# Image loops of two stages written out, and a group norm spread over more taps

## What is computed

```python
x = x + L0(_gn(x), ...)   # state space scan over the 4096 positions of half the channels, 3x3 convolution of the rest
x = x + L1(_gn(x), ...)   # four sweeps of a 9-tap convolution, line by line: down, up, right, left
x = x + L2(_gn(x), ...)   # column convolution times a gate of 8 groups
x = x + L3(_gn(x), ...)   # deformable convolution, batch norm, leaky relu

def _gn(v, G=32, eps=1e-5):          # group norm: mean and variance of 4 channels of one image
    g = v.reshape(B_, G, C_ // G, H_, W_)
    return ((g - mean(g)) / sqrt(var(g) + eps)).reshape(v.shape)

# deformable convolution: offsets and mask from a 3x3 convolution of the input; each of 9 taps reads
# four corners at an offset position, weighs them, and a 128x128 product per tap is summed
samp = corner(y0, x0, ...) + corner(y0, x0 + 1, ...) + corner(y0 + 1, x0, ...) + corner(y0 + 1, x0 + 1, ...)
out = einsum('bckhw,ock->bohw', samp * mask, dcn_w)
```

## Time and profile before

| | |
|---|---|
| three runs | 6858.83, 6863.93, 6866.51 us |
| the profiled execution | 6866.86 us, its span 6865.1 us |
| first stage, about 108 to 2118 us | DVE busy 1906 of 2010 us |
| second layer, 2118 to 3690 us | PE busy 1540 of 1572 us |
| preparing image 0, 3690 to 3821 us | PE busy 117 of 131 us |
| sampling, 3821 to 6765 us | 2304 gathers on POOL |
| the end, 6765 to 6865 us | stores and loads |

### The profile page before, as it was taken

The page is one execution under the profiler, slowest core; times in us unless marked ns, Lnnn a source line. Parts: engine busy times, 40 slices in busy tenths (PEclk is TensorE's granted clock), DMA queues, the critical chain, the costliest instruction groups (busy, mean ns, idle before and its releaser), DMA issues. The chain is left out here.

```text
span 6865.1 us, 89120 instructions
## 1 busy us (share of the span) xinstructions
PE 5560.6 (81%) x21147; PEld 3191.4 (46%) x21147; DVE 5515.3 (80%) x12845; ACT 3422.5 (50%) x7221; POOL 4025.5 (59%) x3805
## 2 busy tenths in 40 slices
PE   4999999999998999999998767667676767676542
PEld 2444444444446888888885323333233333333221
DVE  6999999999996777777885777777878787877667
ACT  4888787888885541111111444444444444444333
POOL 3888888888882000010000577777777777777773
PEclk9999999999999999999999988888897989798665
DMA  5455444444443000000000677777777777777777
GB/s 194 174 186 180 174 166 169 164 178 164 174 167 128 3 4 0 0 25 0 0 0 20 187 244 218 238 222 230 227 227 233 221 240 216 243 211 237 213 209 284
DMA packets 306391, 1093.54 MB, mean 159 GB/s; under 512 B 56560, under 2 KB 58639, under 8 KB 264604
## 3 DMA queue, kind: packets, MB, share of 16 engines
q0 software_dynamic: 187440, 625.23, 30.2%
q1 hardware_dynamic: 118516, 464.08, 18.9%
HBM read 997.72 MB, written 91.37 MB: 159 GB/s over the span
## 5 line engine op out<-in xcount | busy, mean ns | idle before, releaser
L1286 POOL DMA_INDIRECT d_ring<-corner_table,d_idx_now x2304 | 2207.7, 958 | 873.0 <-issue 797.4
L983 POOL TENSOR_TENSOR X<-X 128x512 f32<-128x512 f32 x1024 | 1286.2, 1273 | 235.5 <-DVE X L1021 219.2
L1332 ACT ACTIVATE d_mix<-d_ring,d_w_now 128x128 f32<-128x128 f32 x2304 | 735.9, 390 | 1319.7 <-DMA d_ring<-corner_table,d_idx_now 1243.4
L1486 PE MATMUL d_ps_s<-small,d_mix 128*128 128x128 f32 x2304 | 454.7, 330 | 985.9 <-DVE d_mix L1658 969.8
L1021 DVE TENSOR_TENSOR_SCAN X<-X,m_pB 128x512 f32<-128x512 f32 x896 | 1133.2, 1270 | 0.0
L1658 DVE SCALAR_TENSOR_TENSOR d_acc<-d_ring,d_w_now,d_mix 128x128 f32<-128x128 f32 x2304 | 662.7, 355 | 579.4 <-ACT d_mix L1332 559.9
L277 PE MATMUL prop_ps<-prop_parts,prop_w_hi 128*128 128x480 f32 (+4 forms) x4536 | 1097.4, 386 | 4.6 <-DVE prop_parts L286 4.6
L877 PE MATMUL m_pY<-X,small 128*128 128x512 f32 x2048 | 1033.5, 602 | 73.9 <-POOL X L983 73.7
L1486 PEld LDWEIGHTS d_ps_s<-small,d_mix 128*128 128x128 f32 x2304 | 296.1, 164 | 1524.3 <-DVE d_mix L1658 871.4
L277 PEld LDWEIGHTS prop_ps<-prop_parts,prop_w_hi 128*128 128x128 f32 x4536 | 814.8, 188 | 132.8 <-DVE prop_parts L286 5.4
L225 ACT ACTIVATE prop_sum<-prop_ps 128x256 f32<-128x256 f32 x504 | 194.5, 386 | 1166.7 <-PE prop_ps L277 1166.7
(11 more groups left out here) (231 smaller groups left out, 8047.3 us busy)
## 6 DMA issues: line engine op xcount, KB each, us to landing
X<-c_scratch SPq DMA_DIRECT2D x256, 1024.0 KB, 4.8
d_ring<-corner_table,d_idx_now POOLq DMA_INDIRECT x2304, 3.7
corner_table<-d_tT SPq DMA_DIRECT2D x120, 256.0 KB, 3.9
X<-in_x SPq DMA_DIRECT2D x8, 2048.0 KB, 15.2
m_res<-in_x SPq DMA_DIRECT2D x64, 256.0 KB, 4.5
x_scratch<-m_res SPq DMA_DIRECT2D x64, 256.0 KB, 2.1
x_scratch<-X SPq DMA_DIRECT2D x8, 2048.0 KB, 8.7
b_x<-x_scratch POOLq DMA_DIRECT2D x16, 1024.0 KB, 12.9
```

The source lines that it names most:

```text
L983: pool.tensor_tensor(hc[:, n % NHC, :], h[:, n, :], Cb[:, n, :], ALU.mult).then_inc(s.HC, 1)
L1286: pool.indirect_dma_start(out=ring[:, m % RING, :], out_offset=None, in_=flat, in_offset=bass.IndirectOffsetOnAxis(ap=idx_now[:, c % 2, m: ...
L1332: r0 = act.activation(R[:, k % 3, t, :], ring[:, m % RING, 0:P], ACT.Copy, scale=w_now[:, c % 2, 4 * m:4 * m + 1])
L1486: turned = pe.transpose(ps_s[k % 3][:, t, :], R[:, k % 3, t, :], G.ident)
```

## The change

The loops over images become Python loops, so that all images are straight code on every engine: three places. In the preparation, table and offsets begin two slots later (`T_AT` 34 in place of 32); the steps of each norm are at slots 0, 2 and 3 after its first (28, 30, 31, and 68, 70, 71), PE's average stays one slot after the first, ACT's root is three after it. `add_x1` goes from every 5 slots to every 4 (34, 38, ... 62). The averages of the two norms use two banks. Two waits of PE fall away or are replaced.

```diff
-            with eng.Fori(1, B) as b:            # layer0, program: PE, DVE, ACT, POOL
+            for b in range(1, B):
-                with sp.Fori(1 + KEEP, B - 1) as b:
+                for b in range(1 + KEEP, B - 1):
-                with eng.Fori(1, B - 2) as p:    # layers2_and_3, passes: all engines
+                for p in range(1, B - 2):
-    T_AT = NORM_AT + 4
+    T_AT = NORM_AT + 6
-    NORM_STEPS = ((0, 5), (5, 9), (9, GN))
-    ADD_AT = {T_AT - 1 + 5 * i: i for i in range(NCH)}
-    X1_LOAD = {max(0, 5 * i - 6) // 2: i for i in range(1, NCH)}
-    FIRST_NORM_AT = max(T_INDEX) + 1
+    NORM_STEPS = ((0, (0, 5)), (2, (5, 9)), (3, (9, GN)))
+    ADD_AT = {T_AT + NT * i: i for i in range(NCH)}
+    X1_LOAD = {max(0, NT * i - 4) // 2: i for i in range(1, NCH)}
+    FIRST_NORM_AT = max(T_MASK)
+            ps_moments = (ps_c[:, 0:2], ps_a[:, 0:2])
...
-                            if n == NORM_AT + 2:
+                            if n == NORM_AT + 3:
                                 deviation(q, 1)
-                            if s.adding and n == FIRST_NORM_AT + 2:
+                            if s.adding and n == FIRST_NORM_AT + 3:
                                 deviation(q + 1, 0)
...
-                        pe.matmul(ps_c[:, 0:2], G.group_mean, mom[:], start=True, stop=True).then_inc(s_gm, 1)
+                        pe.matmul(ps_moments[which], G.group_mean, mom[:], start=True, stop=True).then_inc(s_gm, 1)
...
                             if n == NORM_AT + 1:
-                                pe.wait_ge(s_math, NM * NCH * s.q + CREDIT)
                                 group_moments(s.q, 1)
                             if s.adding and n == FIRST_NORM_AT + 1:
-                                pe.wait_ge(s_math, NM * NCH * s.q + NM * NCH + CREDIT)
+                                after(pe, s_mask, NCH * s.q + (NCH - 1))
+                                pe.wait_ge(s_math, NM * NCH * s.q + (NM * (NCH - 1) + 1 + CREDIT))
                                 group_moments(s.q + 1, 0)
...
-                            if i == 0:                     # before PE's first turn of the offsets
-                                after(pe, s_gn, GN * 2 * q + (GN + 8))
...
-                            for later, steps in enumerate(NORM_STEPS):
+                            for later, steps in NORM_STEPS:
                                 if n == NORM_AT + later:
                                     image_norm(s.q, 1, *steps)
```

More of the change, by code:

```diff
@@ L1085, in layers2_and_3 @@
     ALL = NCH * TAPS
-    NORM_STEPS = ((0, 5), (5, 9), (9, GN))
-    ADD_AT = {T_AT - 1 + 5 * i: i for i in range(NCH)}
-    X1_LOAD = {max(0, 5 * i - 6) // 2: i for i in range(1, NCH)}
-    FIRST_NORM_AT = max(T_INDEX) + 1
-    assert max(ADD_AT) < FIRST_NORM_AT and FIRST_NORM_AT + 2 < ALL
+    NORM_STEPS = ((0, (0, 5)), (2, (5, 9)), (3, (9, GN)))
+    ADD_AT = {T_AT + NT * i: i for i in range(NCH)}
+    X1_LOAD = {max(0, NT * i - 4) // 2: i for i in range(1, NCH)}
+    FIRST_NORM_AT = max(T_MASK)
+    assert max(ADD_AT) < FIRST_NORM_AT and max(FIRST_NORM_AT + 3, max(T_TABLE) + 3, max(T_INDEX)) < ALL
     with ExitStack() as ctx:
@@ L1585, in image_norm @@
                             after(dve, s_gm, 2 * q + which)
-                        do(5, lambda: dve.tensor_copy(gm[:], ps_c[:, 0:2]))
+                        do(5, lambda: dve.tensor_copy(gm[:], ps_moments[which]))
                         do(6, lambda: dve.tensor_tensor(mv3[:, 0:1], gm[:, 0:1], gm[:, 0:1], ALU.mult))
@@ L1703, in _ @@
                         add_x1(0, i)
-                    for steps in NORM_STEPS:
+                    for _, steps in NORM_STEPS:
                         image_norm(0, 0, *steps)
```

## The result

The changed kernel takes 6829.51 us, median of six runs (6825.53 to 6831.34), where the kernel before takes 6864.65 beside it (six runs, 6858.83 to 6871.18). The ratio is 0.9947, 95% interval 0.9937 to 0.9958: 0.5% or 35 us faster, with 29 and 43 us as the ends. Forecast were 42 us less and 6822. The profiled execution of the changed kernel has a span of 6828.5 us against 6865.1, 36.6 less.

A forecast was written before the change was run, and what follows sets the result against it. DVE was taken to pace the first stage and POOL's gathers the sampling, no engine being busy throughout. 33.0 + 12.4 - 3.3 = 42.1 us less gave 6821.8 us, range 6801 to 6841.

The forecast's parts named there:

- First stage: DVE-paced first stage: writing out its loops removes 33.0 us, bounds 22.7 and 33.5.
- Both prices: First stage: chunk pairs across a jump fall to 61.46 us, 22.7 less in all; inner chunks to 30.69, 10.1 less.
- The rival that straight code waits for its own fetch: First stage and sampling: straight code pays the loop's price elsewhere, so 6867 us, no change; chance 0.06.
- Sampling loop: Passes 1 to 5: written out, they come to the straight passes' mean, 367.01 us each, 12.4 us less in all.
- the lower bound: Sampling, passes 2 to 5: only the gather queue's stands at four jumps go, 9.8 us.
- Norm steps: Slots 29 and 70: DVE's waits for PE, 40.8 us, go but gain 0; slot 29 at most 21 us.
- Table two slots later: Before the next image's first gather: two slots use 10.0 of 18.7 us of slack, cost 0.
- `add_x1`: Sampling slots shared with the last index steps: DVE 1.3 us late, queue bears 2.2; cost 0, at most 2 us in all.
- The third rival: Passes 0 to 5, 36 slots: bunched adds hold gathers 1.6 us each, 56 us back, 14 us slower, 6878; chance 0.03.
- Pass -1: Preparation before the first gather: adds inside chunks 0 to 5 cost 3.3 us more, bounds 0 and 4.4.
- The ring: Pass -1: PE turn, mask, 13 index steps, next turn take 6.10 us in place of 5.3 where an add falls within.
- its own bounds: Whole kernel: the forecast's own terms and runs differing by 4 us were said to give 6813 to 6829 us.

The follow-up runs named there:

- The schedule in loops: Changed kernel with its three loops put back, leaving only the new norm, table and add slots: 6860.91 us, ratio 0.9995 to the kernel before.
- The runs with the store in pieces: Changed kernel with each image's 2 MB store cut into eight of 256 KB: 6809.2 us; with norm steps in three successive slots too: 6839.48 us.
- the three parts: Kernel before with only first-stage loops written out, 6830.28 us; only the passes loop, 6856.61; changed kernel with all loops put back, 6860.91.

## Why the prediction was right, and where a step failed

**First stage, 33.0 forecast, 34.2 measured.** Of these, 0.8 lie ahead of the first mark of the earlier trace rows (191.90 against 191.09 us), where the code is the same in both. Both prices held on every image, 30.69 us a chunk and 61.35 to 61.40 a pair, and the edit alone takes the same 34.2 us out of the stage. The straight image 0 was the experiment, and it was in the trace of the kernel before. The Trainium skill's figure of about 108 ns for a compare-and-branch (Advanced Engine Details and Errata, Control Flow Timing) would have given 10.3 and an estimated 0.6 us. The run decides against it as the price of a jump here. The rival that straight code waits for its own fetch is out: 64 chunks without such a stop.

**Sampling loop, 12.4 forecast, 7.1 measured.** The stand behind the jump was the right mechanism, the size was not right. The term took passes 1 to 5 down to the mean of passes 0 and 6, 367.0; they came to 368.1. Straight code alone gave 9.3, near the 9.8 that the stands of the gathers had given and that I held as the lower bound. The mean of two passes was too thin a base, when two profiles of the same five passes differ by 3.7 us. The prediction did say that the norm's wait at slot 70 lies within the price of the straight passes. The schedule in loops shows how far: it alone takes 10.8 us out of the same passes, so the 7.1 us can't be put down to the loop rather than to the schedule. That the denser adds cost something is not shown, since passes 1 to 5 take 1841.6 with the adds moved.

**Norm steps, 0 forecast.** Right for slot 29 and by the reason given: the corner of slot 30, late by the image store, ended last (4.97 us of standing for ACT; gather 33 stood as before; the steps put together changed nothing there). The runs with the store in pieces show the cover: taken away, the split matters. Wrong for slot 70. I argued from the old slots, where pass 1 came in at full rate, and did not put the norm's new place, 68 to 71, beside the index steps that end at 70. There the split saves 8 to 10 us that the new slots would else have cost, and in a loop the new schedule, most likely by the split, removes most of the stand after a jump. Neither adds to the sum of the whole change, since the one only makes good what the schedule costs, and the other is the stand that the straight code removes as well.

**Table two slots later, 0; `add_x1`, 0 to 2.** Pass 0 came out 0.03 us shorter, pass 6 0.2 longer. No gather stands at slots 45, 49, ... 65 by more than 0.5 us. The third rival, the slower kernel, is out.

**Pass -1, 3.3 forecast, 3.5 measured where the term lies.** The ring of 6.10 us came five times behind a first one of 6.43, and turn 6 at 36.9 after turn 0 (36.8 forecast, 33.45 before). The 2.9 of the table is counted from where the lower clock had ended, and pass -1 makes up for part of that by turn 0; from PE's first matmul to the first mix it is 4.3. The adds moved by a slot took all of it away again, with all rings short, those of chunks 3 and 4 too (from the first matmul 137.7 us, against 143.0 in the changed kernel and 138.7 before).

**What no step had:** 3.6 us given back in the second layer and the first matmuls behind it, whose code nobody touched, and 2.0 us won in pass 7 and the end. Of the first, the rows put 2.6 us down to the lower TensorE clock (1.6 in nine matmuls, 1.0 in six). The second is in the profile of the kernel before and not in the change: its pass 7 and end take 452.9 us, and 450.4 to 450.6 in the two experiments that have the same code there.

**The sum.** 34.2 and 7.1 and 2.0 won, 3.6 and 2.9 and 0.2 given back: 36.6. So the median is near the forecast because the first stage was priced right; that a term of 12.4 came out as 7.1 and stretches of no term moved by 3.6 and 2.0 is in the same number. The parts measured one by one (37.0, 10.6 and 6.3 us) add to 54 where the whole has 35. The profiles say where: passes 1 to 5 are shorter by 3.7, 9.3 and 10.8 us in the three parts, 23.8 together, and by 7.1 in the changed kernel. The 3.7 is unchanged code, and the other two are the one stand, removed once. With 6 to 9 us on each side of every ratio the rest can't be told. A slip in the prediction belongs here too: its own bounds reach from 6813 to 6836 us (22.7 and 9.8 won, 4.4 given back), not to 6829.

## What to carry to other kernels

A kernel that writes out its first iterations before a loop holds the price of the loop in its own trace: compare the straight iterations with the looped ones, stage by stage, and only where the engine that sets the pace runs the loop. Before a wait is priced, look for what lands last at the same place; here two waits lay over each other, and the bigger gain (15 to 20 us) was in a store whose size could be cut, not in DVE's wait of 40.8 us. When a change has several parts, ask whether two of them remove the same wait. When a step is moved, put its new slots beside everything else that is in these slots, and not only the slots it leaves.

## What the runs showed of the hardware

A loop's jump cost the engine that sets the pace 3.4 to 4.1 us each time (64.75 to 65.5 against 61.4 in the first stage, 4.12 against 0.35 in sampling), and 0.24 us in every chunk of 30.7 inside it, which straight code does not have; neither shows as a busy instruction. The cause of the 0.24 is not shown. For the jump it is: 3 to 5 packets of instructions, of 8 KB, start 1.0 to 1.2 us into the idle time at every one of the six jumps of the first stage. The Trainium skill (Runtime: NRT & Kernel Launch, Instruction fetch mechanics) has a taken branch out of the fetched window wait for a fetch from memory, and straight code mostly without a price. The traces agree with both, and give the size that the page leaves out.

A plain store of 2 MB beside indirect gathers takes 8.9 us to land. While it is under way the gathers move 232 packets in 8.5 us in place of 546, and ACT waits 7.3 to 8.4 us for a corner issued beside it. Eight stores of 256 KB, 2.6 to 4.5 us each, leave stands of at most 1.3 us at slots 32 and 33. And unchanged code is not unchanged time: 1593.35 and 1595.54 us for the same second layer, with nine matmuls in it that take 3.84 us in place of 2.27 at a lower granted clock, and 1847.4 and 1843.7 us for the same five looped passes, without a cause that I know.
